# Causal mask in the rounded format and units in pairs in a first attention stage, and one token rounding moved in a second stage

## The reference, cut to what matters

```python
# x: 8 sequences of 512 tokens, width 128
x = x + causal_attention(layernorm(x))      # stage 1: 16 heads of width 8
u = layernorm(x)                            # stage 2: six layers
for i in range(6):
    u = local_attention(shift(u), Wqkv[i], q_scale[i], k_scale[i], Wo[i]) + u   # 16 heads of 64, window 32
    u = geglu_ffn(shift(u), ln_g[i], ln_b[i], W1[i], b1[i], W2[i], b2[i]) + u
out = x + u
# causal_attention, per head
attn = q @ k.T * 8 ** -0.5
attn = where(causal, attn, -inf)
y = softmax(attn) @ v
```

## Time and profile before

| | us |
|---|---|
| median of 3 runs | 4179.59 |
| lowest and highest | 4172.83, 4183.58 |
| the profiled execution, its own time | 4182.92 |
| its span, first to last instruction | 4181.1 |
| PE busy | 3900.5 (93%) |
| DVE busy | 3305.5 (79%) |
| ACT busy | 3091.6 (74%) |
| POOL busy | 2581.2 (62%) |
| mean granted TensorE clock, of 2.4 GHz | 0.986 |

### The profile page before, as it was taken

The page is one execution under the profiler, slowest core; times in us unless marked ns, Lnnn a source line. Parts: engine busy times, 40 slices in busy tenths (PEclk is TensorE's granted clock), DMA queues, the critical chain, the costliest instruction groups (busy, mean ns, idle before and its releaser), DMA issues.

```text
span 4181.1 us, 190344 instructions
## 1 busy us (share of the span) xinstructions
PE 3900.5 (93%) x78816; PEld 3039.7 (73%) x78816; DVE 3305.5 (79%) x5294; ACT 3091.6 (74%) x10376; POOL 2581.2 (62%) x2583
## 2 busy tenths in 40 slices
PE   6888885999998999989999989999899999899998
PEld 3555554888866888848888668888488887588884
DVE  6778874988866888938888668989489886698894
ACT  5877785888865888838888658888488886588883
POOL 4667765766645676627666456766377664566660
PEclk9999998999999999999999999999999999999999
DMA  1000001111111111111111111111111111111110
GB/s 35 2 2 2 2 2 53 47 45 45 46 56 38 45 47 45 44 50 44 49 44 46 58 36 47 44 49 42 53 44 47 47 44 61 35 45 46 47 43 26
DMA packets 100195, 167.40 MB, mean 40 GB/s; under 512 B 26224, under 2 KB 33648, under 8 KB 99056
## 3 DMA queue, kind: packets, MB, share of 16 engines
q1 hardware_dynamic: 99312, 154.89, 12.6%
HBM read 26.13 MB, written 2.10 MB: 7 GB/s over the span
## 4 chain that ended last, share of the span: by engine, by line
PE 69%; issue 9%; POOL 3%; DVE 1%; ACT 0%; DMA 0%; SPq 0%; POOLq 0%; DVEq 0%; ACTq 0%
PE s_bank L1177 13%; PE s_bank L1246 10%; PE s_bank L1259 9%; PE s_bank L1198 8%; PE s_bank L1157 5%; PE s_proj L1222 4%; PE s_proj L1223 4%; PE s_proj L1224 4%; PE s_bank L1209 2%; PE s_bank L1210 2%; PE s_bank L1211 2%; PE s_bank L1167 2%; PE s_bank L1140 1%; POOL s_rotated L802 1%; PE s_bank L1289 1%
## 5 line engine op out<-in xcount | busy, mean ns | idle before, releaser
L802 POOL TENSOR_TENSOR s_rotated<-s_rotated,s_by_sin 128x512 f32<-128x512 f32 x768 | 983.8, 1302 | 227.3 <-DVE s_by_sin L1087 225.2
L811 POOL TENSOR_TENSOR s_probs<-s_probs,s_rden 128x256 f32<-128x256 f32 x768 | 479.7, 641 | 729.8 <-DVE s_rden L1027 729.3
L901 ACT ACTIVATE s_probs<-s_bank,s_neg_max 128x64 f32<-128x64 f32 x3072 | 908.0, 310 | 5.7 <-DVE s_neg_max L1020 5.6
L783 DVE TENSOR_TENSOR s_qk<-s_rotated,s_inv_norm 128x1024 f32<-128x1024 f32 x384 | 743.8, 1937 | 11.5
L1082 DVE TENSOR_TENSOR s_rotated<-s_proj,s_cos 128x1024 f32<-128x1024 f32 x384 | 469.6, 1223 | 241.5 <-ACT s_sq L935 240.9
L901 ACT ACTIVATION_READ_ACCUMULATOR s_probs<-s_bank,s_neg_max 128x1 f32 x3072 | 636.1, 207 | 0.0
L891 ACT ACTIVATE s_probs_t<-s_bank 64x512 f32<-64x512 f32 x384 | 226.8, 591 | 524.8 <-PE s_bank L1157 524.8
L1177 PE MATMUL s_bank<-s_qk 32*32 32x64 f32 x49152 | 581.4, 223 | 26.3 <-issue 25.9
L1177 PEld LDWEIGHTS s_bank<-s_qk 32*32 32x32 f32 x49152 | 510.9, 103 | 115.4 <-issue 114.6
L213 POOL TENSOR_TENSOR s_probs<-s_probs,s_rden 128x384 f32<-128x384 f32 (+3 forms) x512 | 406.4, 802 | 206.1 <-DVE s_rden L406 202.2
L824 POOL TENSOR_TENSOR s_sq<-s_sq 128x512 f32<-128x512 f32 x384 | 490.2, 1277 | 65.5 <-ACT s_sq L935 59.8
(11 more groups left out here) (118 smaller groups left out, 8156.2 us busy)
## 6 DMA issues: line engine op xcount, KB each, us to landing
s_v<-s_v SPq DMA_DIRECT2D x384, 192.0 KB, 2.5
s_v<-s_v SPq DMA_DIRECT2D x384, 64.0 KB, 2.4
s_qk<-f_wqk SPq DMA_DIRECT2D x6, 1024.0 KB, 6.4
s_xs_raw<-u SPq DMA_DIRECT2D x48, 128.0 KB
s_xf<-u SPq DMA_DIRECT2D x48, 128.0 KB, 2.3
s_xs_raw<-u SPq DMA_DIRECT2D x48, 127.8 KB
s_xf<-u SPq DMA_DIRECT2D x48, 127.8 KB, 2.6
s_qk<-f_wv SPq DMA_DIRECT2D x6, 512.0 KB, 6.8
```

The lines of the kernel that those rows point to most:

```text
L783: return nc.vector.tensor_tensor(qk[:, quad % 2, :, :, at:at + TOKS], rotated[:, par, :, :, :], by, ALU.mult)
L802: nc.gpsimd.tensor_tensor(rotated[:, par, :, half, :], rotated[:, par, :, half, :], by_sin[:, :, 1 - half, :], (ALU.subtract, ALU.add)[half])\
L811: nc.gpsimd.tensor_tensor(part, part, by, ALU.mult).then_inc(S["probs_done"], 1)
L901: last = nc.scalar.activation(probs[:, par, h, b, :], score_bank[h][:, b * KEYS:(b + 1) * KEYS], ACT.Exp, scale=-1.0, bias=neg_max[:, par, ...
```

## The change

In stage 1 the identity and the causal mask are converted to F32R instead of bf16, and the mask matmul reads these. The bodies of `scores` and `transposes` are those that stood in TensorE's `unit` before, and `COPY_LAG` stands in the `unit` of ScalarE and of VectorE. TensorE issues the scores of two units (even step), and in the odd step the transposes of two units, lags 5 and 4. The copies out of the transpose banks stand in the step 5 behind instead of 4, on both engines. In stage 2, ScalarE rounds the tokens of sequence 0 of the next layer after the gates of feed-forward sequence 5; for the first layer it does so ahead of the loop. Since the last layer has no next one, ScalarE's loop runs over five layers and the last is written out behind it.

```diff
+COPY_LAG = TR_LAG + 1
-        ident_b = sb("s1_ident_b", [P, P], BF16)
+        ident_r = sb("s1_ident_r", [P, P], F32R)
-        causal_b = sb("s1_causal_b", [P, P], BF16)
+        causal_r = sb("s1_causal_r", [P, P], F32R)
...
-                of = behind(s, par, t, TR_LAG, first)
+                of = behind(s, par, t, COPY_LAG, first)
...
-            nc.vector.tensor_copy(ident_b[:, :], ident[:, :]).then_inc(S["mask_ready"], 1)
-            nc.vector.tensor_copy(causal_b[:, :], causal[:, :]).then_inc(S["mask_ready"], 1)
+            nc.vector.tensor_copy(ident_r[:, :], ident[:, :]).then_inc(S["mask_ready"], 1)
+            nc.vector.tensor_copy(causal_r[:, :], causal[:, :]).then_inc(S["mask_ready"], 1)
...
+            def scores(s, par, t, first):
...
+                nc.tensor.matmul(score_bank[t % 4][:, n - P:n], ident_r[:, :], causal_r[:, :],
+                                 start=False, stop=True, skip_group_check=True).then_inc(S["score_done"], 1)
+
+            def transposes(of, first):
...
             def unit(s, par, t, first, last):
+                if t < UNITS and t % 2 == 0:
+                    scores(s, par, t, first)
+                    scores(s, par, t + 1, first)
+                if t % 2 == 1:
+                    for lag in (TR_LAG + 1, TR_LAG):
+                        of = behind(s, par, t, lag, first)
+                        if of:
+                            transposes(of, first)
...
+XS_FFN = 5
...
+            def tokens_high(l, of):
+                act.wait_ge(S["xs_in"], (l * NSEQ + of) * 64 + 64)
+                nc.scalar.activation(xs_high[:, of % 2, :], xs_raw[:, :], ACT.Copy).then_inc(S["xs_high"], 1)
...
-                if first and p == 0:
-                    tokens_high(0)
                 if p == XS_STEP and s < NSEQ - 1:
-                    tokens_high(s + 1)
+                    tokens_high(l, s + 1)
...
+            tokens_high(0, 0)
+
+            def layer(l, last):
                 steps(l, step)
...
-                ffn_gate(l * NSEQ + 3)
-                for s in range(4, NSEQ):
+                for s in range(3, NSEQ):
                     ffn_gate(l * NSEQ + s)
+                    if s == XS_FFN and not last:
+                        tokens_high(l + 1, 0)
+
+            if depth > 1:
+                with act.Fori(0, depth - 1) as l:
+                    layer(l, False)
+            layer(depth - 1, True)
```

More of the change, by code:

```diff
@@ L492, in finish @@
                 pe.wait_ge(S["ln_xn"], k + 1)
-            def unit(s, par, t, first, last):
[L495 to L522, removed]
@@ new lines, in scores @@
+            def scores(s, par, t, first):
+                g, b, i = UNIT_LIST[t]
+                if b == 0 and i == 0:
+                    pe.wait_ge(S["diag_vector"], (s * GROUPS + (g + 1)) * len(DIAG_VECTOR))
+                    pe.wait_ge(S["diag_pool"], (s * GROUPS + (g + 1)) * len(DIAG_POOL))
+                    pe.wait_ge(S["k_split"], s * GROUPS + (g + 1))
+                n = P * (b + 1)
+                if not (first and t < 4):
+                    pe.wait_ge(S["exp_done"], s * UNITS + (t - 3))
+                nc.tensor.matmul(score_bank[t % 4][:, 0:n], q_diag[:, par, g * HPG + i, b * P:(b + 1) * P],
+                                 k_t[:, par, g, 0:n], start=True, stop=False, skip_group_check=True)
+                nc.tensor.matmul(score_bank[t % 4][:, n - P:n], ident_r[:, :], causal_r[:, :],
+                                 start=False, stop=True, skip_group_check=True).then_inc(S["score_done"], 1)
@@ new lines, in transposes @@
+            def transposes(of, first):
+                us, _, u = of
+                pe.wait_ge(S["probs_done"], us * UNITS + (u + 1))
+                if u >= 2:
+                    pe.wait_ge(pt(u - 2), pt_count(us, u - 2))
+                elif not (first and u >= 0):
+                    pe.wait_ge(pt(UNITS + u - 2), pt_count(us - 1, UNITS + u - 2))
+                for kb in range(UNIT_LIST[u][1] + 1):
+                    done = nc.tensor.transpose(tr_bank[u % 2][:, kb * P:(kb + 1) * P],
+                                               probs[:, u % N_PROBS, kb * P:(kb + 1) * P], ident[:, :])
+                done.then_inc(S["tr_done"], 1)
@@ L905, in exponentials @@
                     last.then_inc(S["exp_done"], 1)
-                def tokens_high(of):
-                    act.wait_ge(S["xs_in"], (l * NSEQ + of) * 64 + 64)
-                    nc.scalar.activation(xs_high[:, of % 2, :], xs_raw[:, :], ACT.Copy).then_inc(S["xs_high"], 1)
-                if first and p == 0:
-                    tokens_high(0)
                 if p == XS_STEP and s < NSEQ - 1:
-                    tokens_high(s + 1)
+                    tokens_high(l, s + 1)
                 if ln and p == LN_STEP + 2:
@@ L964, in _ @@
             nc.scalar.activation(in_rows(w_high[:, :]), w_raw, ACT.Copy).then_inc(S["w_high"], 1)
-            with act.Fori(0, depth) as l:
+            tokens_high(0, 0)
+            def layer(l, last):
                 steps(l, step)
```

## The result

The changed kernel takes **4210.3 us** (4207.4 to 4214.1, 4 runs) against 4176.2 us of the kernel before on the same chip: ratio 1.008, 95% interval 1.0061 to 1.0098. It is slower by 34 us, and above the whole forecast range (4130 to 4208). The profiled execution took 4212.5 us, its span is 4210.5 us.

A forecast was written before the change was run, and what follows sets the result against it. The first stage was taken as set by engines waiting for each other in strict order, none full; the second as untouched. Terms summed to -2.0 us a sequence, -16 us over 8, giving 4163.5 us, range over the cases 4130 to 4208.

The forecast's parts named there:

- the first rival: First stage, odd units' transposes: their wait for ScalarE's later copies takes over, +13 to +33 us, 4193 to 4212; chance 0.17.
- two signs: First stage: transposes' wait for ScalarE's copies passing 10 us a sequence, and a period above 80.2 us.
- Odd transposes wait for the later copy: First stage, TensorE: 25 of 30 odd units' transposes 0.6 us late, mostly hidden; +1.4 us a sequence, bounds 0 and 15.
- the sum: First stage, one sequence: +0.9 - 1.9 - 2.4 + 1.4 = -2.0 us of 80.2; times 8, -16 us.
- ScalarE still holds two units of work: First stage, when TensorE is let go: some 2 x 0.9 us of ScalarE work hides late transposes, scores and minimum.
- Copies' waits gone: First stage, ScalarE: 2.4 of its copies' 5.3 us wait for transposes goes, -2.4 us a sequence, bounds 0 and 5.3.
- Odd scores earlier: First stage: odd scores precede even transposes, halving VectorE's 3.8 us wait for scores; -1.9 us a sequence, bounds 0 and 3.8.
- the second rival: First stage: VectorE is the bound, so scores come earlier but minima don't; no change, 4172 to 4190; chance 0.36.
- Mask, +0.9: First stage, TensorE: the rounded identity's slower load costs 0.9 us a sequence, +7 us, half of 14.
- The third rival: First stage, TensorE: the mask's load is all on the path, +14 us; 4170 with gains, 4194 without, the latter 0.05.
- Tokens, 0: Second stage, layer boundaries: rounding the next layer's tokens earlier moves work but saves no time, bounds -2 and +2 us.
- Second stage unchanged within 3 us: Sign for the second stage, 3480 of 4181 us: its length stays within 3 us.

The follow-up runs named there:

- q1_duties: Changed kernel, copies still five behind, with ScalarE's table load, key copies and attention output copy moved behind the copy of transposes: 4186.5 us, 1.0022 of the kernel before.
- p3_both_odd: Changed kernel with ScalarE's copies of a pair both in the odd step, even unit's five behind, odd unit's four behind: 4171.9 us, 0.9999 of the kernel before.
- p7_table: Changed kernel with only ScalarE's function table load moved behind the copy of the same step: 4217.4 us, 1.0094 of the kernel before.
- m1_mask: Kernel before with only identity and mask changed to the rounded format: 4178.2 us, 1.0006 of the kernel before.
- p1_lag4: Changed kernel with the copies out of the transpose banks four units behind again, pairs and rounded mask kept: 4205.0 us, 1.0063 of the kernel before.
- t2_first_only: Changed kernel's first stage with the second stage of the kernel before: 4210.8 us, 1.0084 of the kernel before.
- q4_odd_duties: p3_both_odd with ScalarE's other duties also moved behind the copies of the odd step: 4174.0 us, 0.9994 of the kernel before.

## Why the prediction was wrong

The forecast was 4163.5 us; the first rival came true, 4193 to 4212. Its two signs are there: the transposes' wait for ScalarE's copies is 12.2 us, above 10, and the period above 80.2. Its mechanism fits: without half clock a sequence costs 3.3 us more, inside the rival's +1.6 to +4.1. That the whole +34 us comes so near to the rival's upper end of +33 is in part luck, since a third of it is the clock, which the rival didn't count. Step by step:

- **Odd transposes wait for the later copy, +1.4 us a sequence, bounds 0 and 15.** This step failed. It took the wait as hidden but for 1.4 us. Without half clock the new order costs 3.3 us a sequence net of all gains, where the sum had -2.0; with half clock it costs 5.2 (31.1 us over six sequences). Two things in its working were wrong. First, it priced the copy's lateness by the exponential of u+2 alone, 0.6 us on average. ScalarE's strict order holds more between two copies: a table load of 1.28 us, two key copies of 1.37, an output copy of 0.62; waits reach 2.0 us. q1_duties shows what they cost: some 25 of the 34 us, 1.4 of the 3.3 us a sequence by the order and most of the rest by way of the clock. Second, "ScalarE still holds two units of work" held less in sets of 128 columns, which take 1.4 of the 1.9 us that stay in q1_duties. The prediction named this (2 x 0.6 us) as a point for the rival and did not price it; that the shorter work is the reason fits the sets, but no run tests it alone. p3_both_odd gives the odd unit's copy its old distance, and the whole loss goes.
- **The clock.** It was read as 1.00 and held there. No term and no rival had a price for a TensorE that waits more and then runs at half clock: 1.1 to 1.5 us each, 11.4 us in six sequences. In p7_table there is less waiting in one place, and four stretches more; but since equal first stages had nine and eleven, four more can be chance in part.
- **Copies' waits gone, -2.4.** The waits shrank nearly as said (5.3 to 3.2; 1.9 in p3_both_odd), the time did not.
- **Odd scores earlier, -1.9.** In the changed kernel the minima wait longer, since the pair of scores stands behind the waiting transposes. In p3_both_odd the wait fell from 3.8 to 2.4 us, and the period is 80.3 as before: the exponentials wait 14.3 us for minima in place of 10.5. Both gains seem to have passed into that wait, which is what the second rival said. What holds a sequence at 80 us, with no engine full, was not found.
- **Mask, +0.9.** The distances held: 0.11 to 0.14 us, and the load of the rounded identity now takes 191 ns at full clock (198 as the mean of the sequence with half clock in it) where it took 96. The Trainium skill ("TensorE: Matmul & The Clock Gate", section on weight-path perf modes) gives the fast load only to formats other than FP32, and the trace agrees; but by its section on LDWEIGHTS, columns at 1.2 GHz, an estimate for 128 columns is 107 ns, and the trace has 191 for the rounded load. In time m1_mask puts the change at 0.14 us a sequence, so TensorE's waits seem to cover it. The third rival fell.
- **Pairs with the old copies** would, by the prediction's logic, have lost nothing; p1_lag4 lost 26 us. An even unit's transposes move back one step with the pair. The prediction said that the odd scores are the one thing that moves. Seen from ScalarE, whose copy of the even unit stands where it stood, the transposes have moved back behind them, and it waits 11.3 us.
- **Tokens, 0.** Right: 1.0001 (0.999 to 1.0012). **Second stage unchanged within 3 us**: it came out 6 us shorter, less than profiles of equal code differ by; m1_mask, with the second stage of before, has 3459 us where before has 3471.

## What to carry to other kernels

When work moves back in an engine's own order, price it by everything that the engine does between the old place and the new, rare duties included (here table load, key copies), not by the usual neighbour; and look at the distance between a buffer's release and its next use in units, for each kind of unit by itself. A wait that disappears is a gain only if the engine that it held up isn't then held by the next wait: p3_both_odd had 4.8 us less of two waits a sequence (5.3 to 1.9 and 3.8 to 2.4) and the same time. Where TensorE idles more, look at the granted clock in the sets of the changed kernel before crediting any gain or loss to the order.

## What the hardware showed unexpectedly

- Half-clock stretches of 3.4 us in the middle of a steady stage on one core, each stretching its set by 1.1 to 1.5 us; a V projection of two matmuls of 512 columns took 1.91 us in place of 1.02. After 150 us there are none in the kernel before, two with the mask alone, nine in the changed kernel (eleven in t2_first_only, with the same first stage), 13 with the table load moved, none in q4_odd_duties. How busy TensorE was just ahead doesn't tell them: 1.24 us of 3.4 kept the clock, 1.71 lost it.
- A rounded identity's load is twice as long in the records (191 ns against 96) and costs almost nothing in time (1.0006, 0.9997 to 1.0016).
- Outside half clock, and behind the first sequence, a set of four units repeats to 0.01 us, rarely 0.05, from sequence to sequence, so single sets can be compared where whole runs spread by 0.3%.
